# Low parts of the value products moved to GpSimd in two slots, one chunk of the feed-forward part a slot earlier, and another order at the end

## The reference

```python
qkv = xp @ w_qkv
sim = einsum('bhnid,bhnjd->bhnij', qw * scale, kw)      # masked
attn = softmax(sim)
attn = einsum('gh,bhnij->bgnij', w_th, attn)
out = einsum('bhnij,bhnjd->bhnid', attn, vw) @ w_out + b_out
x = layernorm(x + out)
# ternary_linear: rows divided by their root mean square, weights sign(w) * (|w| > alpha/2)
h = gelu(ternary_linear(x, w_up))
x = layernorm(x + ternary_linear(h, w_down))
```

## Time and profile before

| | |
|---|---|
| median of three runs | 239.44 us |
| the profiled execution | 239.48 us |
| its span | 237.7 us |
| mean granted clock of TensorE | 0.981 |
| TensorE busy | 221.2 us (93%) |
| VectorE busy | 177.2 us (75%) |
| ScalarE busy | 168.0 us (71%) |
| GpSimd busy | 100.3 us (42%) |

### The profile page before, as it was taken

How to read it: one execution, slowest core, us unless ns; L and a number is a source line. 1 busy time by engine, 2 the same in 40 slices (tenths; PEclk the granted TensorE clock), 3 DMA queues, 4 the chain that set the end, 5 groups by cost and what they waited for, 6 DMA issues and landing times.

```text
span 237.7 us, 9733 instructions
## 1 busy us (share of the span) xinstructions
PE 221.2 (93%) x4200; PEld 203.5 (86%) x4200; DVE 177.2 (75%) x459; ACT 168.0 (71%) x313; POOL 100.3 (42%) x118
## 2 busy tenths in 40 slices
PE   7999989999999999999999999999999969989880
PEld 7899879888999898999989898989898959978770
DVE  0675799987877975688767966896679787884954
ACT  2686557676666669866997599768986787575671
POOL 7035204513151415761666265724574367212232
PEclk9999999999999999999999999999999988999995
DMA  6947570020002000200021002100101001000002
GB/s 209 286 106 196 174 172 7 3 66 3 3 13 58 26 3 12 59 25 4 11 61 38 14 3 69 40 11 3 57 17 42 3 4 43 26 4 22 3 3 66
DMA packets 19106, 11.67 MB, mean 49 GB/s; under 512 B 2232, under 2 KB 18168, under 8 KB 18936
## 3 DMA queue, kind: packets, MB, share of 16 engines
q1 hardware_dynamic: 18324, 10.47, 15.7%
q10 hardware_dynamic: 740, 0.59, 0.8%
HBM read 8.91 MB, written 2.10 MB: 46 GB/s over the span
## 4 chain that ended last, share of the span: by engine, by line
PE 52%; DVE 14%; issue 14%; ACT 10%; POOL 9%; POOLq 0%; DVEq 0%; ACTq 0%
PE bank L1103 8%; PE bank L1105 7%; PE bank L1104 7%; PE bank L1252 7%; PE bank L1226 6%; PE bank L1210 4%; DVE CTl L879 4%; POOL xw L506 3%; POOL E L519 2%; ACT CTh L584 2%; POOL rstd L549 2%; PE bank L1184 2%; PE bank L1158 2%; ACT y L707 1%; DVE mx L891 1%
## 5 line engine op out<-in xcount | busy, mean ns | idle before, releaser
L519 POOL TENSOR_TENSOR E<-E,rc 128x400 f32<-128x400 f32 x32 | 27.9, 872 | 80.3 <-DVE rc L901 80.3
L879 DVE TENSOR_TENSOR CTl<-bank,CTh 128x512 fp32r<-128x512 f32 x64 | 41.2, 686 | 27.6 <-ACT CTh L584 27.6
L584 ACT ACTIVATE Yb<-bank 128x512 f32<-128x512 f32 x64 | 38.5, 602 | 27.9 <-PE bank L1105 26.7
L584 ACT ACTIVATE CTh<-bank 128x512 fp32r<-128x512 f32 x64 | 34.8, 600 | 8.7 <-PE bank L1252 8.6
L1103 PE MATMUL bank<-xTh,Gh 128*128 128x256 f32 x128 | 39.0, 305 | 0.3 <-DVE Gl L828 0.2
L1103 PE MATMUL bank<-CTh,Mh 128*128 128x256 f32 x128 | 37.1, 290 | 0.5 <-DVE CTl L879 0.5
L1104 PE MATMUL bank<-CTl,Mh 128*128 128x256 f32 x128 | 36.4, 284 | 0.0
L1105 PE MATMUL bank<-CTh,Ml 128*128 128x256 f32 x128 | 36.3, 284 | 0.0
L1104 PE MATMUL bank<-xTl,Gh 128*128 128x256 f32 x128 | 35.8, 280 | 0.0
L1105 PE MATMUL bank<-xTh,Gl 128*128 128x256 f32 x128 | 35.7, 279 | 0.0
L1252 PE MATMUL bank<-AT,xw 50*128 50x256 f32 x384 | 31.1, 294 | 3.3 <-DVE AT L884 3.3
(11 more groups left out here) (143 smaller groups left out, 476.3 us busy)
## 6 DMA issues: line engine op xcount, KB each, us to landing
raw<-in_L_attn_x SPq DMA_DIRECT2D x37, 64.0 KB
pt_rows<-PT SPq DMA_DIRECT2D x2, 512.0 KB, 5.0
R<-pt_rows SPq DMA_DIRECT2D x1, 1024.0 KB, 5.1
xr<-in_L_attn_x SPq DMA_DIRECT2D x6, 128.0 KB
out<-y SPq DMA_DIRECT2D x6, 128.0 KB, 1.9
raw<-in_L_attn_x SPq DMA_DIRECT2D x13, 56.0 KB
w_sb<-in_L_attn_w_qkv SPq DMA_DIRECT2D x2, 256.0 KB, 4.9
w_sb<-in_L_attn_w_qkv ACTq DMA_DIRECT2D x2, 256.0 KB, 4.9
```

Of the source, the lines that this page charges most:

```text
L519: tt(e, e, rc[s % 2][:, :].unsqueeze(2).broadcast_to([P, TILES, WIN]), ALU.mult).then_inc(s_norm, 1)
L584: copy = lambda o, i, **k: nc.scalar.activation(o, i, ACT.Copy, **k)
L879: v.tensor_tensor(ct_view(CTl[s // 4 % 2], s % 4, q), c_view(s, q), ct_view(f32(CTh[s // 4 % 2][:, :, :]), s % 4, q), ALU.subtract).then_i ...
```

## The change

In slots 28 and 30 (`COPIED = (26, 28)`, the value products of slots 26 and 28) ScalarE evacuates each of the two banks twice: a plain copy into a free quarter of `Yb[0]` (`c_copy`) and CTh. GpSimd subtracts them (`values_low`), behind its `normalise`, and VectorE leaves these out. TensorE's next `c_part` waits for the two evacuations.

Chunk 4's steps 1 to 6 come a slot earlier (its step 0 stays in slot 26 and step 1 joins it), with its places in the queues chosen apart (`n == 4`). For chunks 0 to 4 `x1_T`, `x1_hi` and `x1_lo` move from the end of step 1 and the start of step 2 behind the transposes and the shift of step 2, and `up` behind `o_part` and `down`. The lists at the end change: `second_sum(4)` is in slot 30, `hidden_low(6)` is on GpSimd, one half of `hidden_high(7)` on VectorE, `down(6)` behind `up(7)`, `down_back(6)` behind `down(7)`, and there are 16 `keep_busy` matmuls in place of 22. The diff, with little of its context:

```diff
@@ -58,6 +58,7 @@
 TURN = 7
+COPIED = (26, 28)
@@ -290,7 +292,10 @@
-            return [(n, s - first) for n, first in enumerate(FIRST) if -1 <= s - first < (9, 9, 9, 9, 6, 1)[n]]
+            steps = [(n, s - first) for n, first in enumerate(FIRST) if n != 4 and -1 <= s - first < 9]
+            if s >= FIRST[4] - 1:
+                steps += [(4, k) for k in {25: [-1], 26: [0, 1]}.get(s, [s - 25])]
+            return [(n, k) for n, k in steps if n < 5 or k < 1]
@@ -518,6 +527,14 @@
+            def values_low(s):
+
+                for q in range(2):
+                    pool.wait_ge(s_copy, 2 * COPIED.index(s) + 1 + q)
+                    pool.wait_ge(s_CTh, 2 * s + 1 + q)
+                    tt(ct_view(CTl[s // 4 % 2], s % 4, q), c_copy(q).rearrange("p (r h s) -> p r h s", r=2, s=BLK),
+                       ct_view(f32(CTh[s // 4 % 2][:, :, :]), s % 4, q), ALU.subtract).then_inc(s_CTl, 1)
@@ -528,7 +545,9 @@
                 pool.wait_ge(f_gh, 2 * n + t + 1)
-                need(pool, f_dn, n)
+                need(pool, f_dn, 0 if n == 6 else n)
+                if n == 6:
+                    pool.wait_ge(f_gl, 12 + t)
@@ -556,12 +575,16 @@
                         hidden_root(n)
+                    if k == 0 and n == 4:
+                        variance_roots(n)
                 for n, k in ffn(s):
-                    if k == 0:
+                    if k == 0 and n != 4:
                         variance_roots(n)
-                    if k == 6:
+                    if k == 6 and n < 4:
                         last_root(n)
+                if s - 2 in COPIED:
+                    values_low(s - 2)
@@ -573,8 +596,10 @@
             hidden_root(5)
+            hidden_low(6, 0)
+            hidden_low(6, 1)
+            last_root(5)
             hidden_root(6)
-            last_root(5)
@@ -631,6 +656,9 @@
                     act.wait_ge(s_C, 2 * s + 1 + q)
+                    if s in COPIED:
+                        act.wait_ge(s_CTl, 2 * s)
+                        copy(c_copy(q), bank[C_BANK[q]][:, :]).then_inc(s_copy, 1)
@@ -647,15 +675,20 @@
+            add_bias = lambda o, i: nc.scalar.activation(o, i, ACT.Identity, bias=b_sb[:, 0:1])
+
+            def first_column(n):
+
+                need(act, f_aT, n)
+                add_bias(attnS[:, CHUNK - 1:CHUNK], bosT[:, n // 4:n // 4 + 1])
                 need(act, f_aT, n)
-                add_bias = lambda o, i: nc.scalar.activation(o, i, ACT.Identity, bias=b_sb[:, 0:1])
                 else:
-                    add_bias(attnS[:, CHUNK - 1:CHUNK], bosT[:, n // 4:n // 4 + 1])
@@ -723,6 +756,9 @@
                     at_hi(s - 1)
+                for n, k in ffn(s):
+                    if k == 2:
+                        x1_hi(n)
@@ -735,21 +771,25 @@
                 for n, k in ffn(s):
-                    if k == 2:
+                    if k == 2 and n < 4:
                     y_out(s, 1)
+                for n, k in ffn(s):
+                    if k == 2 and n == 4:
+                        gelu(n, 0)
+                        gelu(n, 1)
                     if k == -1:
+                        if n % 4 == 3:
+                            first_column(n)
                         down_out(n)
-                    if k == 1:
-                        x1_hi(n)
@@ -765,8 +805,9 @@
             hidden_high(5, 1)
+            result(4)
             x1_hi(6)
-            result(4)
+            first_column(7)
@@ -778,11 +819,11 @@
             x1_hi(7)
+            gelu(7, 0)
+            gelu(7, 1)
+            act.wait_ge(f_gh, 15)
+            hidden_high(7, 1)
             down_out(6)
-            gelu(7, 0)
-            hidden_high(7, 0)
-            gelu(7, 1)
-            hidden_high(7, 1)
@@ -941,12 +982,15 @@
                 dve.wait_ge(f_gelu, 2 * n + t + 1)
-                need(dve, f_dn, n)
+                dve.wait_ge(f_gh, 2 * n + t)
+                need(dve, f_dn, {7: 5}.get(n, n))
                 dve.wait_ge(f_gh, 2 * n + t + 1)
+                if n == 7:
+                    dve.wait_ge(f_gl, 14 + t)
@@ -959,12 +1003,12 @@
                 dve.wait_ge(f_hroot, n + 1)
-                dve.wait_ge(f_back, n + 1)
                 dve.wait_ge(f_weight, n + 1)
+                dve.wait_ge(f_back, n + 1)
@@ -1003,18 +1047,18 @@
             for s in range(STEPS):
-                for n, k in ffn(s):
-                    if k == 2:
-                        x1_lo(n)
                     at_lo(s - LAG)
-                if s > TURN:
+                if s > TURN and s - 2 not in COPIED:
                 shift(s)
+                for n, k in ffn(s):
+                    if k == 2:
+                        x1_lo(n)
@@ -1024,9 +1068,13 @@
                 for n, k in ffn(s):
-                    if k == 1:
+                    if k == 1 and n < 4:
                         up_input(n)
+                    if k == 0 and n == 4:
+                        residual(n)
+                    if k == 5 and n == 3:
+                        second_sum(n)
@@ -1037,8 +1085,11 @@
                 for n, k in ffn(s):
-                    if k == 5 and n < 4:
+                    if k == 5 and n != 3:
                         second_sum(n)
+                    if k == 1 and n == 4:
+                        input_scale(n)
+                        up_input(n)
@@ -1063,19 +1114,16 @@
             x1_lo(5)
-            second_sum(4)
+            second_norm(4)
             ct_lo(31)
-            second_norm(4)
             result_shift(4)
-            hidden_low(5, 0)
             up_input(6)
+            hidden_low(5, 0)
             residual(7)
-            hidden_low(6, 0)
-            hidden_low(6, 1)
@@ -1083,6 +1131,7 @@
             hidden_sum(6)
+            hidden_high(7, 0)
@@ -1240,7 +1289,12 @@
                 pe.wait_ge(s_ATl, s + 1)
-                need(pe, s_CTl, 2 * s)
+                if s - 1 in COPIED:
+                    pe.wait_ge(s_CTl, 2 * s - 2)
+                    pe.wait_ge(s_copy, 2 * COPIED.index(s - 1) + 2)
+                    pe.wait_ge(s_CTh, 2 * s)
+                else:
+                    need(pe, s_CTl, 2 * s)
@@ -1358,8 +1412,7 @@
                     if k == 2:
-                        up(n, 0)
-                        up(n, 1)
+                        x1_T(n)
@@ -1373,10 +1426,14 @@
                         down(n)
+                    if k == 2 and n < 4:
+                        up(n, 0)
+                        up(n, 1)
                 for n, k in ffn(s):
-                    if k == 1:
-                        x1_T(n)
+                    if k == 2 and n == 4:
+                        up(n, 0)
+                        up(n, 1)
@@ -1401,16 +1458,16 @@
             down_back(5)
-            keep_busy(1, 4)
-            down(6)
+            keep_busy(1, 8)
             square_sum(6)
-            down_back(6)
-            keep_busy(1, 4)
+            keep_busy(1, 2)
             up(7, 1)
-            keep_busy(1, 14)
+            down(6)
+            keep_busy(1, 6)
             down(7)
+            down_back(6)
```

More of the change, by code:

```diff
@@ L196, in attention_ffn @@
         s_O = sem("s_O")
+        s_copy = sem("s_copy")
         s_xr = [sem("s_xr"), sem("s_xr_last")]
@@ L350, in f32, with c_copy @@
             return ap.bitcast(F32)
+        def c_copy(q):
+            return Yb[0][:, 4 * q:4 * q + 4, :].rearrange("p a b -> p (a b)")
         block = ctx.enter_context(nc.Block())
```

## The result

The changed kernel takes **246.77 us** (median of 4 runs, 245.69 to 248.65) beside 239.62 us (239.44 to 240.01, 4 runs) of the kernel before: a ratio of 1.030 with a 95% interval of 1.0235 to 1.0373. I had 241.2 us and a range up to 244.3. The direction was right, the size was not: the loss is 7.2 us in place of 1.7, and the median lies 5.6 us over the forecast.

A forecast was written before the change was run, and what follows sets the result against it. TensorE, busy 93% of the span, was taken as the bound, with GpSimd's queue deciding slots 28 and 29. Against 239.48 us, -1.8 + 6.1 - 2.6 = +1.7 gave 241.2 us; own range 239.5 to 243.5, with rivals 237.9 to 244.3.

The forecast's parts named there:

- Step 1: Moving `x1_T` and `up` later removes TensorE's waits for `x1n` and AT up to slot 27: -1.8 us.
- Step 2: Slots 26 and 27: chunk 4 a slot early costs nothing, as the normalised E still comes in time.
- Steps 3 and 4: Slots 28 and 29: ScalarE's evacuations make `normalise(28)` 2.0 us later; GpSimd's queue idles TensorE 5.2 us at `down(4)`.
- Step 5: Slots 30 and 31: lower clock, then TensorE idles 0.8 us; with the earlier losses `up(5)` comes 6.1 us later.
- Step 6: The new end, with `hidden_low(6)` on idle GpSimd and VectorE freed, is shorter: -2.6 us.
- A: Rival: GpSimd is not late at `down(4)`, so idle time and low clock go too: 231.5 us; chance of ending faster 0.17.
- B: Rival: gains and the wait at `down(4)`, near 4 us, cancel: 239.5 to 240.1 us; chance 0.11.
- D: Rival: ScalarE's four evacuations alone bound, slot 29 only 2 us late: 237.1 us; within the chance of A.
- C: Rival: clock stays low between gaps of slots 28 to 31 and the end's start, 2 to 3 us more: 244; chance 0.15.

The follow-up runs named there:

- e_wait: The changed kernel, with GpSimd starting `hidden_low(6)` only when both halves of `x1n(7)` are written; 245.51 us, ratio 1.028.
- e_rows27: The changed kernel with `rows_low(7)` moved to the end of slot 27 on GpSimd, ahead of the queue; 244.68 us, ratio 1.024.
- b_steady: The kernel before with only the moves of `x1_T`, `x1_hi`, `x1_lo` and `up`; 236.79 us, ratio 0.990.
- c_wait: c_steady_end, with GpSimd starting `hidden_low(6)` only when `x1n(7)` is done; 235.19 us, ratio 0.982.
- c_dve6: c_steady_end with `hidden_low(6)` back on VectorE, behind `residual(7)`; 235.76 us, ratio 0.988.
- d_nocopy: The changed kernel without the copies (`COPIED = ()`), chunk 4 still a slot early; 243.26 us, ratio 1.019.
- w_copies_rows27: c_wait with the copies in both slots and `rows_low(7)` at the end of slot 27; 235.34 us, ratio 0.986.
- c_steady_end: The changed kernel without copies and with chunk 4 as before, so the steady moves and the new end; 236.84 us, ratio 0.990.
- d_rows27_wait: d_nocopy with `rows_low(7)` at the end of slot 27 and `hidden_low(6)` waiting for `x1n(7)`; 238.84 us, ratio 1.000.
- f_copies_unpressed: The changed kernel with its copies but chunk 4 as before (c_steady_end with `COPIED = (26, 28)`); 239.69 us, ratio 1.002.
- e_low4_dve: The changed kernel with `hidden_low(4)` on VectorE behind `at_lo(28)`, in place of GpSimd; 245.34 us, ratio 1.025.

## Why the prediction was wrong in size

**Step 1 (-1.8): right, a little large.** It measured -1.1 at slot 26 (0.27 of the rest was there at 57.9 us already, ahead of every moved instruction) and as a whole kernel -2.8, since its shorter gap in slot 29 also saves the low clock. I had kept that gain out: with chunk 4 pressed there is none. What became late next was E, as foretold, but by 0.19 to 0.27 us in six slots, 1.4 us in all, and not by 0.1 in two.

**Step 2 ("Nothing", slots 26 and 27): failed.** I followed VectorE's queue to `total(27)` and never asked what `up(4)` itself waits for. `up` overwrites what `second_sum` of the chunk before still reads, and pressing put `second_sum(3)` and `up(4)` into one slot: 1.07 us. `x1n(4)` ran beside GpSimd's cast `rows_high(7)` and took 1.05 us in place of 0.60: 0.45 us. Together 1.5 of slot 27's 2.1 us over the 7.04 that my times give it (175.71 to 182.75).

**Steps 3 and 4: right.** `down(4)` waited 4.72 us (I had 5.2), released by GpSimd's gTl, behind 0.70 + 2.53 + 2.35 + 2.51 us in the order I gave. Slot 28 came out at 4.34 against 5.15, slot 29 at 12.10 against 12.1. ScalarE's part was smaller than I had it (`c_part(27)` waited 0.48, not 1.4, and `transposes(28)` 0.92, not 1.15), which fits a slot 27 that was itself 2 us longer and took up that lateness. The instruction ahead of the table load ends at 187.45, the load starts at 187.47, and Exp follows 1.29 us after its start. The trace thus disagrees once more with the 1.38 us of drain of the Trainium skill ("ScalarE: Activation LUTs", What ACT_TABLE_LOAD costs).

**Step 5 (+6.1): its mechanism right, 2.4 short.** Slot 30 took 5.92 (6.0). From the start of slot 31 to `c_part(31)` it took 9.97 against my 8.9 (206.0 to 214.9), since `c_part(30)` waits on the semaphore of the low parts, into which `values_low(28)` counts: 1.13 us. I had followed `values_low(28)` only into GpSimd's `normalise(31)`, and the 0.8 us of idle time that I put there did not come. Slots 26 and 27 over by 2.2, slot 28 short by 0.8 and this 1.1 make up the miss.

**Step 6 (-2.6): failed, the largest miss, 4.3 us in the profile.** "`hidden_low(6)` goes to GpSimd, idle there" is the term. It ran beside `x1n(7)` and held it for 0.96 us, TensorE had 0.68 and 0.95 us without work within 3.0, and the clock was at 1.2 GHz from 231 to 238 us. Without the stop (e_wait) the end takes 26.8 us, so the stop and the clock are 2.9 of the 4.3, the stop 0.9 and the clock 2.0 (e_rows27). In an execution whose clock stays up the miss is thus some 2 us smaller. The other 1.4 is size: the order of the end gains 1.3 (b_steady 27.9, c_wait 26.6) and not 2.6. Counted from `up(5)`, `x1_T(7)` comes 1.0 us earlier in c_wait than before (I had 0.85 for `x1n(7)`), but `x1_lo(7)` 0.5 and not 1.2, `up(7)` 1.1 and not 1.8, and the last gTl 1.5 and not 2.6. Even there GpSimd's pair is in VectorE's way: the small `floor` (128x2) ahead of `x1_lo(7)` takes 0.76 us in place of 0.15. I had a sign of it in the trace before. `x1n` took 1.00 us there in place of 0.60, beside a `normalise`, and I read the 0.60 row alone:

```profile
204.89 0.86 POOL L519 TENSOR_TENSOR E<-E,rc 128x400 f32<-128x400 f32 x1 [0.65 <-DVE rc L901]
205.09 1.00 DVE L934 TENSOR_SCALAR x1n<-res,mv,scales 128x128 f32<-128x128 f32 x2
```

I had weighed the rule on contention from its shorter form and priced it at GpSimd's side, 0.5 us. The direction I did not price was VectorE's.

The runs show first: VectorE 0.60 to 1.56 and 1.29 to 3.79, each held until the large GpSimd instruction beside it ends. The Trainium skill ("SBUF — State Buffer", Who interferes with whom) says that VectorE shares one pair of ports with GpSimd as an exclusive lock. A VectorE instruction with two SBUF inputs contends for it, and so can a `tensor_scalar` between SBUF tensors, in a mode that uses both ports; there the one that comes second "fully blocks". The traces agree for these instructions. VectorE's `y`, which has one input in a bank, took its usual 0.61 beside the same GpSimd pair in c_wait. Beside small GpSimd instructions they did not show it: `x1n(7)` took 0.60 us beside an `hroot` (before, and in c_wait), and a `roots` (128x4) that started 0.01 us ahead of a gTl pair (221.22 before) left it at 1.33 us against 1.29. The other way round VectorE held them: two `roots` that started 0.08 us behind a gTl took 1.47 in place of 1.01 (213.92 before, 218.10 in c_dve6).

**The rivals.** A (the freed VectorE wins) and B (cancel) fell with the wait of 4.72 us, over A's 3.5. D (ScalarE's evacuations alone) fell too: without any copy on ScalarE `down(4)` still waits 2.27 + 0.49 for GpSimd (d_nocopy), and with all of them, but `rows_low(7)` out of the way, the time is within 0.15 us of c_wait by the medians, 0.9 by the ratios (w_copies_rows27). C, the clock, is half right: it was low in slots 29 and 30 as forecast and came back, and it fell again in the end, but behind gaps of the end's own, not from those of slots 28 to 31: in e_wait, without the second gap, it stayed at full level from `up(5)` to 237.5 us.

**What each part is worth** (differences of medians; parts overlap):

| part | us | from |
|---|---|---|
| steady moves | -2.8 | b_steady, before |
| new end as written | 0 | c_steady_end, b_steady |
| new end, `x1n(7)` free | -1.6 | c_wait, b_steady |
| chunk 4 pressed, no copies | +6.4 | d_nocopy, c_steady_end |
| the same, both cures | +3.7 (+4.4 by ratios) | d_rows27_wait, c_wait |
| copies, not pressed | +2.85 | f_copies_unpressed, c_steady_end |
| copies, pressed | +3.5 (+2.8 by ratios) | after, d_nocopy |
| copies, `rows_low(7)` moved | +0.15 (+0.9 by ratios) | w_copies_rows27, c_wait |

Open: the last 3.7 us of pressing. The profiles of d_rows27_wait and c_wait differ by 4.0 us. Slot 26 began 0.8 us later in the first (168.26 against 167.45), but as much is there at `c_part(5)` already (58.23 against 57.45), ahead of every slot in which the two kernels differ. So it is no cost of pressing. From slot 26 to `up(5)` it is 42.23 against 39.12 us. Of these 3.1, TensorE's idle time is 2.2 (4.60 against 2.38; the waits are listed at d_rows27_wait), and 0.9 is busy time with as many matmuls (736 and 735) at full clock, for which I have no cause. A `second_sum(3)` ahead of `up(4)` in time, which would take the wait of 1.09, was not tried.

## What to carry to other kernels

An idle engine is not free: before moving an instruction to GpSimd, look at what VectorE does at that moment, and whether those instructions have all their operands in SBUF; a wait on GpSimd that keeps the two apart can gain time. When a step is moved, list what it waits for itself (who still reads what it overwrites, which counter holds the new instruction) besides the queues that it passes. When a queue decides, ask first which of its entries can go earlier: moving one 2.4 us entry to the slot before took away most of the cost of the copies.

## What the runs showed of the hardware

- These VectorE instructions with all operands in SBUF are held until a large GpSimd instruction beside them ends: `x1n` pair 0.60 to 1.56 us (beside gTl), 1.05 (beside the cast) and 1.00 (beside a `normalise`), gTl pair 1.29 to 3.79 (beside xw). GpSimd lost less in the same meeting (xw 2.35 to 2.80). Beside an `hroot` of 128x2 `x1n` kept its 0.60. VectorE's CTl, with one input in a bank, took its usual 1.27 beside GpSimd's CTl pair (191.02 in the changed kernel).
- Two TensorE gaps of 0.68 and 0.95 us within 3.0 us were followed by the lower clock in the profiles of after, c_steady_end and d_nocopy, for 6.4 to 7 us, for some 3.5 us in that of f_copies_unpressed, and not at all in those of e_rows27 and e_low4_dve. With 0.68 and 0.28 us (c_wait) the clock stayed. The same gaps can thus give either level, and a kernel that has them spreads: 3.2 us between executions of c_steady_end, 0.4 in c_wait.
